# The square root moved to the head of the routing loop's turn, and the recurrent weights loaded into four buffers

## Chip, cores and metric

The kernel runs on the 8 cores of one Trainium2 chip. Times are device microseconds (us) of the slowest core. The two measured runs of the kernel before took 2318.80 and 2323.91 us, median 2321.36. The cores share no work: each computes everything that its own 2048 output rows need. Line numbers (L746) are those of the kernel file of the version spoken of.

## What is computed

One layer over x of shape (2, 8192, 1024), cut to what matters here:

```python
xn = layernorm(x)
s  = attn_block(xn)                  # linear attention, MLP with 4096 hidden columns
# slot block, on the same xn
h      = gelu(concat[xn, slot_mean] @ w1 + b1)        # 512 columns
logits = (h @ w2 + b2) / (|tau| + 0.1)                # 64 slots
alpha  = softmax over the 8 largest logits, 0 elsewhere
si = (alpha.T @ xn) / alpha.sum(0)                    # 64 x 1024 per batch
gi = si @ Wih.T + bih ; gh = S @ Whh.T + bhh          # 64 x 3072 each
S_new = GRU(gi, gh, S)
y  = layernorm(S_new + attention(S_new)) * ln_g + ln_b
slot_values = y @ wvp + bvp
g  = silu((alpha @ slot_values) @ wo + bo)
x  = x + s * g
```

`si` sums over all 8192 rows of a batch. A core therefore reads all 8192 rows, of which only the first 2048 are its own.

## The kernel before, in words

The program is a row of blocks. In a block each engine has its own hand-written list of instructions, ordered against the others by semaphores: `sdv` counts VectorE's (DVE) signals, `sac` ScalarE's (ACT), `spe` TensorE's (PE); `swA`, `swc0`, `swc1` count DMAs that GpSimd (POOL) issues. At the end of a block all engines meet.

**The routing stage** (L505 to L812) is one block with a loop over 16 tiles of 512 rows, `mt` = 0 to 15. Tiles 0 to 3 are the core's own (`own`). One turn, engine by engine:

- DVE waits for the square root of tile mt, then runs `emit_stats(mt+1)` (bn_stats and bn_aggr of the next tile, L523 to L530), `emit_apply(mt)` (reciprocal L538, then the four normalizing operations L550, into XN for own tiles, into xnb otherwise) and `emit_tail(mt-1)` (top 8, threshold mask and, after the exponentials, the weights alpha: L565 to L602). For a tile that isn't own, `emit_apply(mt)` first waits for the slot sum of tile mt-2 on PE.
- ACT runs `emit_exp(mt-1)` (L725, L734), which needs the top 8 of that tile from DVE; then `emit_sqrt(mt+1)` (L746); for own tiles four copies XN to xnb (L767); four evacuations of transposes (L777); four Gelus (L786); the copy of the logits, LOG (L795); and once per own tile a copy ALPHAT (L801), one turn late. Sqrt of tile 0 stands ahead of the loop. The loads of ACT's function tables are instructions of their own in the trace (ACT_TABLE_LOAD).
- PE transposes the tile (L675), multiplies by w1 (L689, 32 matmuls), makes the logits (L703, L709), and then sums the slots of tile mt-1 (`emit_si`, L632 to L637).
- SyncE loads tile m of x when tile m-2 has been applied.

The counts that a wait names (`a_sqrt`, `a_copy`, `aoff`, AB) are worked out ahead from the order of ACT's signals.

**The slot stage** (L862 to L1327) has 64 rows only and streams weights. Its first block (L900) only issues loads on POOL: five bias rows (`ROWB3`), slotT, wq, wk and the first two of the eight pieces of Whh, each 128 rows by 3072 columns, float32 in HBM and cast to bf16 on the way. The second block (L923) multiplies piece after piece (L944), six matmuls each, and adds the bias row (L952); POOL loads piece c into buffer c % 2 of `whb` once PE has finished piece c-2. The third block (L965) does the same with Wih (L988, L996). Three more blocks (L1125, L1218, L1276) stream wv, wvp and wo in pieces of 1024 columns.

Of the kernel before, what the change touches and what calls it, by code (L numbers as in the profile page):

```python
# [76 lines left out]
def build_nc(dbg=False):  # L77
# [51 lines left out]
    with ExitStack() as ex:  # L129
# [18 lines left out]
        sfq = E(nc.semaphore("sfq"))  # L148
        sx = [sx0, sx1]; swc = [swc0, swc1]; sfc = [sfc0, sfc1]
# [6 lines left out]
                 al1=0, fq=0)  # L156
# [29 lines left out]
        def fin(inst, sem, key):  # L186
            inst.then_inc(sem, 1)
            C[key] += 1
# [69 lines left out]
        with ExitStack() as exW:  # L258
# [6 lines left out]
            with ExitStack() as exA:  # L265
# [175 lines left out]
                t_c = 0  # L441
                a_c = 1
                for m in range(N_MT):
                    VB.append(v_c); TB.append(t_c); AB.append(a_c)
                    v_c += ((1 if m + 1 < N_MT else 0) + 4
                            + (2 if m >= 1 else 0))
                    t_c += 9 + (0 if m == 0 else
                                1 + (1 if own_f(m - 1) else 0))
                    a_c += ((0 if m == 0 else 1)
                            + (1 if m + 1 < N_MT else 0)  # L450
                            + (4 if own_f(m) else 0) + 9
                            + (1 if m >= 1 and own_f(m - 1) else 0))
# [26 lines left out]
                aoff = lambda m: ((0 if m == 0 else 1)  # L479
                                  + (1 if m + 1 < N_MT else 0)  # L480
                                  + (4 if own_f(m) else 0))
                a_sqrt = lambda m: ac0 + (1 if m == 0 else
                                          AB[m - 1]
                                          + (0 if m == 1 else 1) + 1)
                a_copy = lambda m, st: (ac0 + AB[m]
                                        + (0 if m == 0 else 1)
                                        + (1 if m + 1 < N_MT else 0)
                                        + st + 1)
# [16 lines left out]
                with nc.Block() as blk:  # L505
# [213 lines left out]
                    def _(a):  # L719
# [151 lines left out]
            with ExitStack() as exB3:  # L871
                EB = exB3.enter_context
                ROWB3 = EB(nc.sbuf_tensor("ROWB3", [1, 9216], BF16))
                slotb = EB(nc.sbuf_tensor("slotb", [64, 1024], F32))
                slotTb2 = EB(nc.sbuf_tensor("slotTb2", [128, 512], BF16))
                whb = EB(nc.sbuf_tensor("whb", [128, 6144], BF16))
# [20 lines left out]
                wslot = lambda c: whb[:, (c % 2) * 3072:(c % 2) * 3072 + 3072]  # L897
                wslot1k = lambda c: whb[:, (c % 2) * 1024:(c % 2) * 1024 + 1024]

                with nc.Block() as blk:  # L900
                    @blk.sync
                    def _(s):
                        dma(s, slotb[:], slot_d[:], sld, 'ld')

                    @blk.gpsimd
                    def _(g):
                        dmx(g, ROWB3[0:1, 0:3072], bih_rd[:], swA, 'wA')
                        dmx(g, ROWB3[0:1, 3072:6144], bhh_rd[:], swA, 'wA')
                        dmx(g, ROWB3[0:1, 6144:7168], fbv_rd[:], swA, 'wA')
                        dmx(g, ROWB3[0:1, 7168:8192], bvp_rd[:], swA, 'wA')  # L910
                        dmx(g, ROWB3[0:1, 8192:9216], fbo_rd[:], swA, 'wA')
# [11 lines left out]
                with nc.Block() as blk:  # L923
                    peS = C['pe']
                    wcB = [X['wc0'], X['wc1']]

                    @blk.gpsimd
                    def _(g):
                        for c in range(2, 8):
                            g.wait_ge(spe, peS + c - 1)  # L930
                            cast_load(g, wslot(c), whhT_d, 1, 3072,
                                      src_row0=c * 128,
                                      sem=swc[c % 2], key='wc%d' % (c % 2))

                    @blk.tensor
                    def _(t):
                        t.wait_ge(sld, ldB0)
                        t.wait_ge(swA, wA_B0)
                        for c in range(8):
                            t.wait_ge(swc[c % 2],  # L940
                                      wcB[c % 2] + 16 * (c // 2 + 1) - 16)
                            i = None
                            for jc in range(6):
                                i = t.matmul(  # L944
                                    pGH[:, jc * 512:(jc + 1) * 512],
                                    slotTb2[:, c * 64:(c + 1) * 64],
                                    wslot(c)[:, jc * 512:(jc + 1) * 512],
                                    start=(c == 0), stop=False)
                            fin(i, spe, 'pe')
                        i = None  # L950
                        for jc in range(6):
                            i = t.matmul(pGH[:, jc * 512:(jc + 1) * 512],  # L952
                                         cONE[0:1, 0:64],
                                         ROWB3[0:1, 3072 + jc * 512:
                                               3072 + (jc + 1) * 512],
                                         start=False, stop=True)
                        fin(i, spe, 'pe')
# [7 lines left out]
                with nc.Block() as blk:  # L965
                    peS = C['pe']
                    wcB2 = [X['wc0'], X['wc1']]

                    @blk.gpsimd
                    def _(g):  # L970
                        cast_load(g, wslot(0), wihT_d, 1, 3072, src_row0=0,
                                  sem=swc[0], key='wc0')
                        cast_load(g, wslot(1), wihT_d, 1, 3072, src_row0=128,
                                  sem=swc[1], key='wc1')
                        for c in range(2, 8):
                            g.wait_ge(spe, peS + c - 1)
                            cast_load(g, wslot(c), wihT_d, 1, 3072,
                                      src_row0=c * 128,
                                      sem=swc[c % 2], key='wc%d' % (c % 2))

                    @blk.tensor
                    def _(t):
                        for c in range(8):
                            t.wait_ge(swc[c % 2],
                                      wcB2[c % 2] + 16 * (c // 2 + 1))
# [7 lines left out]
                            fin(i, spe, 'pe')  # L993
                        i = None
# [130 lines left out]
                with nc.Block() as blk:  # L1125
# [4 lines left out]
                    def _(g):  # L1130
                        cast_load(g, wslot1k(0), fwv_d, 1, 1024, src_row0=0,
# [10 lines left out]
                    def _(t):  # L1142
                        for c in range(8):
# [9 lines left out]
                            fin(i, spe, 'pe')  # L1153
                        i = None
                        for nh in range(2):
                            i = t.matmul(pGH[:, nh * 512:(nh + 1) * 512],
                                         cONE[0:1, 0:64],
                                         ROWB3[0:1, 6144 + nh * 512:
                                               6144 + (nh + 1) * 512],
# [58 lines left out]
                with nc.Block() as blk:  # L1218
# [4 lines left out]
                    def _(g):  # L1223
                        cast_load(g, wslot1k(0), wvp_d, 1, 1024, src_row0=0,
# [23 lines left out]
                    def _(t):  # L1248
                        t.wait_ge(sdv, dvS + 1)
                        for c in range(8):  # L1250
# [8 lines left out]
                            fin(i, spe, 'pe')  # L1259
                        i = None  # L1260
                        for nh in range(2):
                            i = t.matmul(pGH[:, nh * 512:(nh + 1) * 512],
                                         cONE[0:1, 0:64],
                                         ROWB3[0:1, 7168 + nh * 512:
                                               7168 + (nh + 1) * 512],
# [10 lines left out]
                with nc.Block() as blk:  # L1276
# [4 lines left out]
                    def _(g):  # L1281
                        cast_load(g, wslot1k(0), fwo_d, 1, 1024, src_row0=0,
# [15 lines left out]
                    def _(t):  # L1298
                        t.wait_ge(sdv, dvS + 1)
                        for c in range(8):  # L1300
# [9 lines left out]
                            fin(i, spe, 'pe')  # L1310
                        i = None
                        for nh in range(2):
# [3 lines left out]
                                         ROWB3[0:1, 8192 + nh * 512:  # L1316
                                               8192 + (nh + 1) * 512],
# [797 lines left out]
```

## Time and profile before

| | |
|---|---|
| measured runs | 2318.80 and 2323.91 us, median 2321.36 |
| profiled execution | 2325.78 us |
| its span, slowest core (core 1) | 2324.2 us |
| spans of the eight cores | 2301.3 to 2324.2 us, granted clock 0.752 to 0.760 |
| PE busy | 1221.8 us, 53% of the span |
| DVE busy | 534.0 us, 23% |
| ACT busy | 502.8 us, 22% |
| routing loop on core 1 | about 94 to 596 us |
| slot stage on core 1 | about 600 to 858 us |

The span runs from the first to the last instruction of the slowest core. In a timeline row the first number is the start in us from the start of the span, the second the length in us, then engine, line and operation; in square brackets stand the idle time of the engine just before and what ended it. Rows with "xN" join N instructions. PEld is the weight load of TensorE. In a row of windows there stand the stretch, its length, for each engine its busy time and in brackets the number of its instructions, and at the end the granted clock as a share of 2.4 GHz, the busy share of the 16 DMA engines, and GB/s. A row of waits gives total us, how many times, and the longest.

### The profile page before, as it was taken

What the parts mean: (1) busy time and instruction counts of PE and PEld (TensorE: products, weight loads), DVE (VectorE), ACT (ScalarE), POOL (GpSimd) and SP (SyncE); (2) the same over time, 40 slices, a digit from 0 to 9 for tenths busy, and PEclk for the clock granted to TensorE, in tenths of its full rate; (3) what the DMA queues carried; (4) which work ended last, traced back from release to release, by engine and by line L of the source; (5) the groups of instructions that cost most, each with busy time, mean ns of one, the idle gap of its engine ahead of it and who ended that gap; (6) DMA issues with size and microseconds to landing.
All of it is one profiled execution on the core that took longest, in us unless ns stands there. A gap on an engine that the chain in (4) does not pass through costs nothing. (4 is left out here: it accounts for less than half of the span.)

```text
span 2324.2 us, 18897 instructions; the slowest of 8 cores (2301.3 to 2324.2 us)
## 1 busy us (share of the span) xinstructions
PE 1221.8 (53%) x6308; PEld 560.4 (24%) x6308; DVE 534.0 (23%) x1213; ACT 502.8 (22%) x747; POOL 122.3 (5%) x139
## 2 busy tenths in 40 slices
PE   0155555555243226447347348340298598697686
PEld 0022222222111002223223213210143243243342
DVE  0242333332001103233233232310400300301002
ACT  0165444444001001101001001000330521521421
POOL 1000000000100110000000000013001001001000
PEclk9977777777665557778678679575599799799798
DMA  9221212220463351512522423339809619439156
GB/s 183 52 96 60 74 49 73 73 72 1 68 120 64 51 80 40 124 38 75 105 63 68 87 64 86 68 91 135 128 1 111 142 19 110 126 37 123 58 55 91
DMA packets 341425, 183.65 MB, mean 79 GB/s; under 512 B 305171, under 2 KB 309396, under 8 KB 341332
## 3 DMA queue, kind: packets, MB, share of 16 engines
q0 software_dynamic: 182144, 72.72, 27.4%
q1 hardware_dynamic: 159188, 109.74, 16.9%
q8 instruction: 53, 0.87, 0.2%
q14 instruction: 40, 0.33, 0.0%
HBM read 204.81 MB, written 33.56 MB: 103 GB/s over the span
## 5 line engine op out<-in xcount | busy, mean ns | idle before, releaser
L689 PE MATMUL pM<-xnTs,w1ab 128*128 128x512 bf16 x512 | 150.8, 464 | 44.6 <-ACTq L191 44.5
L1937 DVE TENSOR_TENSOR y1t<-pTf,y1t 128x512 f32<-128x512 f32 x32 | 22.1, 692 | 520.1 <-PE pTf L2031 520.1
L2000 PE MATMUL pMa<-h2T,fcwb 128*128 128x512 bf16 x512 | 127.7, 394 | 19.4 <-ACTq L191 19.4
L2000 PE MATMUL pMb<-h2T,fcwb 128*128 128x512 bf16 x512 | 123.8, 386 | 0.0
L2017 PE MATMUL pPb<-g1F,pjcb 128*128 128x512 bf16 x512 | 119.2, 393 | 8.7 <-DMA pjcb<-pjw 8.5
L2017 PE MATMUL pPa<-g1F,pjcb 128*128 128x512 bf16 x512 | 113.1, 379 | 9.8 <-DMA pjcb<-pjw 4.9
L1600 ACT ACT_TABLE_LOAD x4 | 5.1, 1283 | 508.3 <-PE pBig L1553 508.3
L675 PE MATMUL pT<-cIDb,xnb 128*128 128x128 bf16 x256 | 27.5, 273 | 163.6 <-ACTq L191 148.7
L1984 PE MATMUL pT0d<-cIDb,h2b 128*128 128x128 bf16 x128 | 16.3, 307 | 159.0 <-DVEq L191 98.2
L689 PEld LDWEIGHTS pM<-xnTs,w1ab 128*128 128x128 bf16 x512 | 57.0, 115 | 134.8 <-issue 101.4
L1858 POOL DMA_DIRECT2D pjcb<-pjw x32 | 53.6, 1676 | 611.1 <-PE pPa L2017 475.7
L1437 PE MATMUL pBig<-wob,aoT 128*128 128x512 bf16 x256 | 67.5, 424 | 27.1 <-DVEq L191 27.1
L1719 PE MATMUL pBig<-FQ2h,FK2h 64*128 64x128 bf16 x256 | 31.7, 298 | 87.5 <-DMA scr_ao<-aog 78.8
L1545 PE MATMUL pBig<-wqb,xhT 128*128 128x512 bf16 x256 | 66.4, 418 | 16.4 <-ACTq L191 16.4
L550 DVE TENSOR_SCALAR xnb<-xld,ST 128x1024 bf16<-128x1024 f32 x48 | 39.0, 812 | 156.2 <-PE pDE L637 151.8
L1763 DVE TENSOR_TENSOR AMK<-pBig,cMSK 128x512 bf16<-128x512 f32 x64 | 44.3, 692 | 130.6 <-PE pBig L1719 100.3
L2000 PEld LDWEIGHTS pMa<-h2T,fcwb 128*128 128x128 bf16 x512 | 51.0, 100 | 84.0 <-issue 27.8
L2017 PEld LDWEIGHTS pPb<-g1F,pjcb 128*128 128x128 bf16 x512 | 50.8, 101 | 72.4 <-issue 19.3
L1839 POOL DMA_DIRECT2D fcwb<-fcw x32 | 28.1, 927 | 735.2 <-DMA y1scr<-XN 699.3
L2000 PEld LDWEIGHTS pMb<-h2T,fcwb 128*128 128x128 bf16 x512 | 51.1, 100 | 63.8 <-issue 6.0
L2017 PEld LDWEIGHTS pPa<-g1F,pjcb 128*128 128x128 bf16 x512 | 49.1, 98 | 70.4 <-issue 13.6
L2059 ACT ACTIVATE h2T<-pT0d,LNC 128x128 bf16<-128x128 bf16 x128 | 58.9, 460 | 27.2 <-PE pT0d L1984 15.3
(263 smaller groups left out, 1729.7 us busy)
## 6 DMA issues: line engine op xcount, KB each, us to landing
xld<-x8k SPq DMA_DIRECT2D x64, 512.0 KB, 7.0
pjcb<-pjw POOLq DMA_DIRECT2D x32, 1024.0 KB, 10.8
scr_qk<-tmb SPq DMA_DIRECT2D x16, 512.0 KB, 2.7
y1scr<-XN SPq DMA_DIRECT2D x4, 2048.0 KB, 7.2
fcwb<-fcw POOLq DMA_DIRECT2D x32, 256.0 KB, 19.1
y1t<-y1scr SPq DMA_DIRECT2D x4, 2048.0 KB, 11.2
xre<-x8k SPq DMA_DIRECT2D x16, 512.0 KB, 12.7
out<-xre SPq DMA_DIRECT2D x16, 512.0 KB, 3.2
```

Source lines behind the costliest of these rows:

```text
L550: i = v.tensor_scalar(dstx, xs, ST[:, pb + 2 * st:pb + 2 * st + 1], ST[:, rd + st:rd + st + 1], ALU.subtract, ALU.mult)
L675: i = t.transpose(dstb[:, cc * 128:(cc + 1) * 128], xb[:, cc * 128:(cc + 1) * 128], cIDb[:])
L689: i = t.matmul(dstp[:, 0:512], w1ab[:, cc * 512 + ch * 128: cc * 512 + (ch + 1) * 128], xnTs[:, cc * 512:(cc + 1) * 512], start=(cc == 0), ...
L1437: i = t.matmul(pBig0[:, nh * 512:(nh + 1) * 512], aoT[:, cc * 128:(cc + 1) * 128], wob[:, cc * 1024 + nh * 512: cc * 1024 + (nh + 1) * 512 ...
L1545: i = t.matmul(pBig0[:, nh * 512:(nh + 1) * 512], xhT[:, cc * 512 + st * 128: cc * 512 + (st + 1) * 128], wqb[:, cc * 1024 + nh * 512: cc ...
L1719: i = t.matmul(pBig0[:, (b % 2) * 512 + gl * 128: (b % 2) * 512 + (gl + 1) * 128], FK2h[0:64, g * 128:(g + 1) * 128], FQ2h[0:64, g * 128:( ...
L1763: i = v.tensor_tensor(AMK[:, (b % 2) * 512:(b % 2 + 1) * 512], pBig0[:, (b % 2) * 512:(b % 2 + 1) * 512], cMSK[:], ALU.mult)
L1839: g.dma_start(out=dstap, in_=srcap).then_inc(sfc[q % 2], 16)
L1858: g.dma_start(out=dstap, in_=srcap).then_inc(spj[slot], 16)
L2000: i = t.matmul(dstp[:, :], fcwb[:, m * 1024 + cc * 128: m * 1024 + (cc + 1) * 128], h2T[:, cc * 512:(cc + 1) * 512], start=(cc == 0), stop ...
L2017: i = t.matmul(dstp[:, :], pjcb[:, (d % 2) * 4096 + m * 128: (d % 2) * 4096 + (m + 1) * 128], g1F[:, m * 512:(m + 1) * 512], start=(m == 0 ...
L2059: i = a.activation(h2T[:, cc * 512 + st * 128: cc * 512 + (st + 1) * 128], pT0d[:, cc * 128:(cc + 1) * 128], AF.Identity, bias=LNC[:, 24 + ...
```

## The change

In the routing stage ACT no longer computes the square root of the next tile between the exponentials and the evacuations. It computes that of the tile of the current turn, ahead of `emit_exp(mt-1)`. The counts are adapted to it. DVE's, PE's and SyncE's lists stay as they are.

In the slot stage `whb` holds four pieces of 3072 columns where it held two (with two more semaphores, `sxt0` and `sxt1`), and `ROWB3` shrinks from 9216 to 3072 columns. The first block loads one bias row and four pieces of Whh; the four other bias rows are each loaded at the head of the block that uses them, and PE waits for them ahead of the bias matmuls. The three streams of 1024-column pieces keep two buffers.

```diff
@@ routing stage, ACT
-                        def emit_sqrt(m):
-                            a.wait_ge(sdv, v_aggr(m))
-                            pb = P_(m); sd = SD_(m)
+                        for mt in range(N_MT):
+                            own = own_f(mt)
+                            par = mt % 2
+                            a.wait_ge(sdv, v_aggr(mt))
+                            pb = P_(mt); sd = SD_(mt)
                             i = a.activation(
...
-                        emit_sqrt(0)
-                        for mt in range(N_MT):
-                            own = own_f(mt)
-                            par = mt % 2
                             if mt >= 1:
                                 emit_exp(mt - 1)
-                            if mt + 1 < N_MT:
-                                emit_sqrt(mt + 1)
@@ slot stage, buffers
-                wslot = lambda c: whb[:, (c % 2) * 3072:(c % 2) * 3072 + 3072]
+                wslot = lambda c: whb[:, (c % 4) * 3072:
+                                      (c % 4) * 3072 + 3072]
+                swc4 = [swc0, swc1, sxt0, sxt1]
@@ first block
-                        dmx(g, ROWB3[0:1, 0:3072], bih_rd[:], swA, 'wA')
-                        dmx(g, ROWB3[0:1, 3072:6144], bhh_rd[:], swA, 'wA')
...
+                        dmx(g, ROWB3[0:1, 0:3072], bhh_rd[:], swA, 'wA')
...
-                        cast_load(g, wslot(0), whhT_d, 1, 3072, src_row0=0,
-                                  sem=swc[0], key='wc0')
-                        cast_load(g, wslot(1), whhT_d, 1, 3072, src_row0=128,
-                                  sem=swc[1], key='wc1')
+                        for c0 in range(4):
+                            cast_load(g, wslot(c0), whhT_d, 1, 3072,
+                                      src_row0=c0 * 128,
+                                      sem=swc4[c0], key=wk4[c0])
@@ second block
-                        for c in range(2, 8):
-                            g.wait_ge(spe, peS + c - 1)
+                        for c in range(4, 8):
+                            g.wait_ge(spe, peS + c - 3)
@@ third block
+                        dmx(g, ROWB3[0:1, 0:3072], bih_rd[:], swA, 'wA')
+                        for c in range(4):
                             cast_load(g, wslot(c), wihT_d, 1, 3072,
                                       src_row0=c * 128,
...
+                        t.wait_ge(swA, X['wA'])
@@ blocks of wv, wvp, wo, each with its own row
+                        dmx(g, ROWB3[0:1, 0:1024], fbv_rd[:], swA, 'wA')
```

ACT's order in the routing stage, before, from the logits of tile 5 to those of tile 6 (L746 is the square root, L725 and L734 the exponentials, L777 the evacuations, L786 the Gelus):

```order
L795 ACTIVATE LOG<-pLb 128x256
L725 ACTIVATE E<-TKS,ST,SCAL 128x8 x4
L734 ACTIVATE etk<-LOG,ST,SCAL 128x64 x4
L746 ACTIVATE ST<-ST,SCAL 128x4
L777 ACTIVATE xnTs<-pT 128x8x128
L777 ACTIVATE xnTs<-pM 128x8x128 x2
L777 ACTIVATE xnTs<-pT 128x8x128
L786 ACTIVATE hFs<-pM,B1E 128x512 x4
L795 ACTIVATE LOG<-pLa 128x256
```

The same stretch in the changed kernel, with its own line numbers (L742 is the square root, L719 and L728 the exponentials):

```order
L784 ACTIVATE LOG<-pLb 128x256
L742 ACTIVATE ST<-ST,SCAL 128x4
L719 ACTIVATE E<-TKS,ST,SCAL 128x8 x4
L728 ACTIVATE etk<-LOG,ST,SCAL 128x64 x4
L766 ACTIVATE xnTs<-pT 128x8x128
L766 ACTIVATE xnTs<-pM 128x8x128 x2
L766 ACTIVATE xnTs<-pT 128x8x128
L775 ACTIVATE hFs<-pM,B1E 128x512 x4
L784 ACTIVATE LOG<-pLa 128x256
```

The square root moved from behind the exponentials to ahead of them, and it is now that of tile 6, the tile whose normalization follows, where before it was that of tile 7.

POOL's order at the start of the slot stage, before (an UNCONDITIONAL_BRANCH marks the entry or the end of a block):

```order
L905 UNCONDITIONAL_BRANCH
L183 DMA ROWB<-bih_r 1x16x192
L183 DMA ROWB<-bhh_r 1x16x192
L183 DMA ROWB<-fbv_r 1x16x64
L183 DMA ROWB<-bvp_r 1x16x64
L183 DMA ROWB<-fbo_r 1x16x64
L200 DMA slotTb<-slotT 128x8x64
L200 DMA fwqb<-fwq 128x8x256
L200 DMA fwkb<-fwk 128x8x256
L200 DMA whb<-whhT 128x3072 x2
L900 UNCONDITIONAL_BRANCH
L927 UNCONDITIONAL_BRANCH
```

And now:

```order
L897 UNCONDITIONAL_BRANCH
L184 DMA ROWB<-bhh_r 1x16x192
L201 DMA slotTb<-slotT 128x8x64
L201 DMA fwqb<-fwq 128x8x256
L201 DMA fwkb<-fwk 128x8x256
L201 DMA whb<-whhT 128x3072 x4
L892 UNCONDITIONAL_BRANCH
L915 UNCONDITIONAL_BRANCH
```

Four bias rows left the first block, and two more pieces of Whh stand in it, ahead of the place where the engines meet.

## Rows read from the trace of the kernel before

**Rows 1.** The longest waits, whole program: who waited, for whom, us, times, longest.

```profile
DVE xnb L550 <- PE pDE L637: 151.8, 12, 17.1
```

**Rows 2.** Windows from the logits of one tile to those of a later one.

```profile
129.78:219.82 90.04, 47.41 (x285) 25.22 (x286) 31.59 (x95) 55.78 (x78) 0.00 (x0) 0.72 0.20 71
219.82:279.72 59.90, 32.34 (x201) 16.37 (x200) 23.24 (x66) 29.12 (x45) 0.00 (x0) 0.74 0.21 71
279.72:556.82 277.10, 149.49 (x865) 72.82 (x864) 99.28 (x285) 125.72 (x189) 0.00 (x0) 0.73 0.19 61
```

**Rows 3.** Timeline of ACT, one turn of the routing loop (tile 8).

```profile
341.68 0.39 ACT L795 ACTIVATE LOG<-pLb 128x256 f32<-128x256 f32 x1 [1.89 <-PE pLb L709]
348.70 1.28 ACT L725 ACT_TABLE_LOAD   x1 [6.64 <-DVEq L191]
...
352.72 1.28 ACT L746 ACT_TABLE_LOAD   x1
...
354.47 1.02 ACT L777 ACTIVATE xnTs<-pT 128x1024 bf16<-128x1024 bf16 x1 [0.16 <-issue]
...
371.86 0.39 ACT L795 ACTIVATE LOG<-pLa 128x256 f32<-128x256 f32 x1 [1.89 <-PE pLa L709]
```

**Rows 4.** Timeline of DVE in the same turn.

```profile
343.63 3.62 DVE L550 TENSOR_SCALAR xnb<-xld,ST 128x1024 bf16<-128x1024 f32 x4 [11.54 <-PE pDE L637]
...
356.97 0.69 DVE L523 BATCH_NORM_STATS2 ST<-xld 128x6 f32<-128x512 f32 x1 [1.10 <-ACTq L191]
```

**Rows 5.** Timeline of ACT and DVE at the first tile.

```profile
101.06 0.30 ACT L746 ACTIVATE ST<-ST,SCAL 128x4 f32<-128x4 f32 x1
101.61 0.69 DVE L523 BATCH_NORM_STATS2 ST<-xld 128x6 f32<-128x512 f32 x1 [1.95 <-ACTq L191]
...
107.32 0.81 DVE L550 TENSOR_SCALAR XN<-xld,ST 128x1024 f32<-128x1024 f32 x1
```

**Rows 6.** Timeline of ACT, own tile 2: logits, ALPHAT copy, first copy.

```profile
158.57 0.39 ACT L795 ACTIVATE LOG<-pLb 128x256 f32<-128x256 f32 x1 [1.73 <-PE pLb L709]
160.76 0.59 ACT L801 ACTIVATE ALPHAT<-pT 64x512 bf16<-64x512 bf16 x1 [1.81 <-PE pT L644]
...
167.32 1.06 ACT L767 ACTIVATE xnb<-XN 128x1024 bf16<-128x1024 f32 x1 [0.21 <-issue]
```

**Rows 7.** Timeline of POOL in the slot stage.

```profile
600.63 0.49 POOL L183 DMA_DIRECT2D ROWB<-bhh_r  x1
...
630.91 0.53 POOL L200 DMA_DIRECT2D whb<-whhT  x1 [24.57 <-PE pGH L944]
...
673.64 1.05 POOL L200 DMA_DIRECT2D whb<-wihT  x2 [15.68 <-DVEq L965]
```

**Rows 8.** Timeline of PE in the slot stage.

```profile
627.61 4.41 PE L944 MATMUL pGH<-whb,slotTb 128*64 128x512 bf16 x12 [28.84 <-PEq L900]
...
667.90 1.48 PE L952 MATMUL pGH<-ROWB,cONE 1*64 1x512 bf16 x6
682.05 2.74 PE L988 MATMUL pGH<-whb,siTb 128*64 128x512 bf16 x6 [12.67 <-DMA whb<-wihT]
686.79 2.74 PE L988 MATMUL pGH<-whb,siTb 128*64 128x512 bf16 x6 [2.01 <-DMA whb<-wihT]
...
723.82 2.76 PE L996 MATMUL pGH<-ROWB,cONE 1*64 1x512 bf16 x6
```

**Rows 9.** Timeline of all engines at the block behind the slot stage.

```profile
858.83 0.90 POOL L200 DMA_DIRECT2D wob<-wo  x1 [7.55 <-PEq L1379]
...
876.10 0.69 DVE L234 BATCH_NORM_STATS2 ST<-XN 128x6 f32<-128x512 f32 x1 [18.07 <-PEq L1379]
```

**Rows 10.** DMA issues: KB and us to landing.

```profile
wob<-wo POOLq DMA_DIRECT2D x1, 2048.0 KB, 15.8
```

**Rows 11.** Timeline of PE, the matmuls by w1 in one turn.

```profile
359.58 9.60 PE L689 MATMUL pM<-xnTs,w1ab 128*128 128x512 bf16 x32 [2.92 <-ACTq L191]
...
360.39 0.15 PEld L689 LDWEIGHTS pM<-xnTs,w1ab 128*128 128x128 bf16 x1 [0.28 <-issue]
```

More of the change, by code:

```diff
@@ L148, in build_nc @@
         sfq = E(nc.semaphore("sfq"))
+        sxt0 = E(nc.semaphore("sxt0")); sxt1 = E(nc.semaphore("sxt1"))
         sx = [sx0, sx1]; swc = [swc0, swc1]; sfc = [sfc0, sfc1]
@@ L440, in build_nc @@
                 v_c = 1
-                t_c = 0
-                a_c = 1
+                t_c = a_c = 0
                 for m in range(N_MT):
@@ L478, in build_nc @@
                 t_alphat = lambda m: pe0 + TB[m + 1] + 11
-                aoff = lambda m: ((0 if m == 0 else 1)
-                                  + (1 if m + 1 < N_MT else 0)
+                aoff = lambda m: (1 + (0 if m == 0 else 1)
                                   + (4 if own_f(m) else 0))
[L482 to L488, printed above, removed]
+                a_sqrt = lambda m: ac0 + AB[m] + 1
+                a_copy = lambda m, st: (ac0 + AB[m] + 1
+                                        + (0 if m == 0 else 1) + st + 1)
                 a_evac = lambda m, st: ac0 + AB[m] + aoff(m) + st + 1
@@ L924, in build_nc @@
                     peS = C['pe']
-                    wcB = [X['wc0'], X['wc1']]
+                    wcB = [X[k] for k in wk4]
                     @blk.gpsimd
                     def _(g):
-                        for c in range(2, 8):
-                            g.wait_ge(spe, peS + c - 1)
+                        for c in range(4, 8):
+                            g.wait_ge(spe, peS + c - 3)
                             cast_load(g, wslot(c), whhT_d, 1, 3072,
                                       src_row0=c * 128,
-                                      sem=swc[c % 2], key='wc%d' % (c % 2))
+                                      sem=swc4[c % 4], key=wk4[c % 4])
                     @blk.tensor
@@ L939, in _ @@
                         for c in range(8):
-                            t.wait_ge(swc[c % 2],
-                                      wcB[c % 2] + 16 * (c // 2 + 1) - 16)
+                            t.wait_ge(swc4[c % 4],
+                                      wcB[c % 4] + 16 * (c // 4))
                             i = None
@@ L966, in build_nc @@
                     peS = C['pe']
-                    wcB2 = [X['wc0'], X['wc1']]
+                    wcB2 = [X[k] for k in wk4]
                     @blk.gpsimd
                     def _(g):
[L971 to L976, printed above, removed]
+                        dmx(g, ROWB3[0:1, 0:3072], bih_rd[:], swA, 'wA')
+                        for c in range(4):
                             cast_load(g, wslot(c), wihT_d, 1, 3072,
                                       src_row0=c * 128,
-                                      sem=swc[c % 2], key='wc%d' % (c % 2))
+                                      sem=swc4[c], key=wk4[c])
+                        for c in range(4, 8):
+                            g.wait_ge(spe, peS + c - 3)
+                            cast_load(g, wslot(c), wihT_d, 1, 3072,
+                                      src_row0=c * 128,
+                                      sem=swc4[c % 4], key=wk4[c % 4])
                     @blk.tensor
@@ L983, in _ @@
                         for c in range(8):
-                            t.wait_ge(swc[c % 2],
-                                      wcB2[c % 2] + 16 * (c // 2 + 1))
+                            t.wait_ge(swc4[c % 4],
+                                      wcB2[c % 4] + 16 * (c // 4 + 1))
                             i = None
@@ L1153, in _ @@
                             fin(i, spe, 'pe')
+                        t.wait_ge(swA, X['wA'])
                         i = None
@@ L1259, in _ @@
                             fin(i, spe, 'pe')
+                        t.wait_ge(swA, X['wA'])
                         i = None
@@ L1310, in _ @@
                             fin(i, spe, 'pe')
+                        t.wait_ge(swA, X['wA'])
                         i = None
```

31 lines of the change are left out of this document (15 added, 16 removed).

## Prediction

> **What bounds the kernel now.** I read the table of cores first: the eight spans lie within 1%, so one core stands for all, and no core waits for another. The page's shares say little, since each stage has its own limit; the change touches two, the routing loop and the slot stage, so I went to the waits. The longest wait of DVE in the routing loop is 151.8 us, twelve times ahead of the normalization L550, for the slot sum on PE [rows 1]. It looks like slack, and the change is about what is in that slack.
>
> Next the windows: nine turns from tile 5's logits to tile 14's take 277.10 us, 30.79 each [rows 2], while in them PE is busy 149.5 us, ACT 125.7 and DVE 99.3. None is full. The turn is a chain through all three. Followed in one turn: logits copied at 341.68; DVE starts to normalize at 343.63, released by PE's slot sum; ACT's table load for the exponentials starts at 348.70, released by DVE (the top 8 of the tail stand behind the normalization in DVE's list); then comes the square root's table load at 352.72, and the first evacuation at 354.47, then transposes, matmuls, Gelus, and the next logits at 371.86 [rows 3, 4]. That is 30.18 us. The reader is to see two things in it. The next tile's statistics start at 356.97, behind the tail, and run beside the matmuls by w1: they cost nothing. And the square root stands on the chain, from 352.72 to 354.47, 1.75 us.
>
> The slot stage is bound by loads: its PE rows wait for DMA between pieces [rows 8].
>
> **The routing stage.** The square root of tile mt now stands behind the logits of tile mt-1 in ACT's list. DVE's list is unchanged: it waits for that root, and *then* does the statistics of tile mt+1, the normalization of mt, and the tail of mt-1. Queued behind the new wait are therefore the statistics, which were hidden, and with them the tail, the exponentials on ACT and all that follows. From the start of the logits copy to the start of the normalization the chain becomes:
>
> 0.39 (the copy) + 0.16 (issue) + 1.28 (table load) + 0.02 + 0.55 (from the root's start to DVE's start of the statistics, 101.06 to 101.61) + 5.71 (statistics to normalization, 101.61 to 107.32) = 8.11 us [rows 3, 5].
>
> Before it was 343.63 - 341.68 = 1.95 us, so 6.16 longer. The root leaves its old place, which gives back 1.75. Net 4.41 us a turn, and 30.18 + 4.41 = 34.59 us for a turn.
>
> - Tiles 6 to 14, nine turns: 9 x 34.59 = 311.3 against 277.1, so +34.2. (Some turns before took longer than 30.18 as their mean of 30.79 shows; where that comes from a later slot sum, it is now covered by the statistics, so I don't add to those.)
> - Tiles 4 and 5: the ALPHAT copy stands ahead of the root. It ends at 160.76 + 0.59 = 161.35, 2.78 us after the logits' start instead of 0.39 [rows 6]. That is 2.39 more, so 4.41 + 2.39 = 6.8 each: +13.6 against the 59.9 us of those two turns [rows 2].
> - Own tiles 2 and 3: before, statistics and normalization of the tile ran ahead in the previous turn, so the way from logits to the first copy was only 167.32 - 158.57 = 8.75 us [rows 6]. Now it is 8.11 + 2.39 to the normalization, + 5.07 to the table load of the exponentials (343.63 to 348.70) + 4.02 through them (348.70 to 354.47, less 1.75) = 19.59 [rows 3, 4]. +10.84 each, 21.7. Tile 1 has no ALPHAT copy ahead; I take 1.2 off for it, half of 2.39, since before part of that copy was hidden: +9.6. Together +31.3, on the 90.04 us of these three turns.
> - Tile 15 has no next tile: no statistics, no root given back. Logits to normalization is 0.39 + 0.16 + 1.28 + 0.02 + 0.55 + 0.25 for the reciprocal (an estimate) = 2.65 instead of 1.95: +0.7. Tile 0 is as before.
>
> Sum: 34.2 + 13.6 + 31.3 + 0.7 = **+79.8 us**. One table load more in all (the first two roots shared one) is within it. x arrives earlier than needed: SyncE loads tile m when m-2 is normalized, and its statistics now start a whole turn later. Bounds: the delays of the chain are read from rows, but the clock of the 32 matmuls by w1 is not fixed; they take 9.60 us [rows 11], and a turn with a different pause ahead of them may take 1 us less or more. 15 turns: 65 to 95.
>
> **The slot stage.** In the third block two loads are issued at 673.64 and their pieces used at 682.05 and 686.79: 8.4 us to the first and 4.74 for the next, with the queue never empty [rows 7, 8]. With four in the queue I take 4.74 for each that follows. The block then runs 673.64 + 0.5 (bias row's issue, 0.49 [rows 7]) + 8.4 + 7 x 4.74 + 2.74 + 2.76 = 721.2, against 723.82 + 2.76 = 726.6: -5.4.
>
> The Trainium skill bears on the 4.74, in DMA: Bandwidth & Descriptors, section "Anatomy of one DMA — SWDGE (gpsimd) path": about 2.0 us and then the bytes at 436 GB/s. By it 1.5 MB would move in 3.6 us, and the block would gain 8 us more. The trace's 4.74 decides here.
>
> In the first block, what releases PE? PE starts both pieces 0 and 1 in one run of 12 matmuls at 627.61, released by the end of the block, not by one piece [rows 8]. And the block behind the slot stage shows the same: wo is issued at 858.83 and lands 15.8 us later, at 874.6, and only then, at 876.10, does DVE leave the block, though its next work needs no wo [rows 9, 10]. So a block's end waits for the loads that POOL issued in it. Then four pieces in the first block hold all engines for two pieces more: 627.61 + 2 x 4.74 - 1.95 (four fewer bias rows at 0.49) = 635.1. POOL issued piece 2 3.3 us after PE's start (630.91); now that is piece 4, at 638.4, into an empty queue. It lands 8.4 later, three more follow at 4.74: 661.0. Then 2.74 + 2.76 at the lower clock, or about half of it at the higher (667.90 shows 1.48): 665.2 in the middle, against 669.38: -4.2. If the end of the block did not wait, the eight pieces would stream through and the gain would be some 12; if loads in the same queue hinder each other, nothing. The three later blocks each issue a bias row first: 3 x 0.5 = +1.5.
>
> Slot stage: -5.4 - 4.2 + 1.5 = **-8.1 us**, bounds -20 and +2. PE, which waits for bias rows now, waits for what landed long before.
>
> **Sum.** 2325.8 (the profiled execution; span 2324.2 and 1.6 around it) + 79.8 - 8.1 = 2397.5. This execution lay 4.4 above the median of the runs, so against the median I take a little less: **2395 us**, 3.2% slower. What can be told from no change is about 2% (46 us).
>
> **Rivals.**
>
> 1. *The clock stays low.* PE's pause ahead of a turn's work grows by 4 to 11 us. In the row of the 32 matmuls the weight loads early in the row come 0.43 us apart (0.15 + 0.28), yet the row takes 9.60, so the clock rises within it. Were it not to rise any more, 32 x 0.43 = 13.8, 4.2 more in 15 turns: +63, **2458 us**. For: the granted clock is only 0.73 in these turns [rows 2, 11]. Against: the pause ahead of these matmuls themselves, from transposes to evacuations, hardly changes. The Trainium skill, TensorE: Matmul & The Clock Gate, section "HAM oscillation — how this bites in real kernels", says that a wait between bursts sends the array back to half rate and each burst starts cold; the trace agrees that each of these turns starts cold already, and so that rule speaks for no new loss.
> 2. *The end of a block doesn't wait for loads*, and PE starts piece 0 when it lands. Then the second block gains 12 instead of 4: **2387 us**. For: piece 0 has its own semaphore. Against: rows 9.
> 3. *Faster.* DVE's 151.8 us ahead of L550 swallow the statistics, and only the root's 1.75 us leave the chain. Place: the gap from the end of the statistics to the normalization. Price: 14 x 1.75 = 24.5 saved, with the slot stage's 8.1: **2293 us**. It decides if the root's result reaches DVE 5.7 us before the slot sum ends. For: the idle time is there, 11.5 us in a turn [rows 4]. Against: ACT reaches the root only after the logits copy, which starts 1.95 us before the slot sum is through, so DVE cannot use the idle time. I see no way round that in ACT's list.
> 4. *Less than it looks*: own tiles hide part of it (DVE's or ACT's slack elsewhere) and the slot stage gains 20: 2325.8 + 60 - 20 = **2366 us**, just within 2%.
>
> **How the numbers follow.** My forecast 0.79, rival 1 0.06, rival 2 0.09, rival 3 0.02, rival 4 0.04. The range of the forecast is 65 to 95 and -20 to +2 around 2321 to 2326, where both ends at once are unlikely: 2372 to 2418, and it takes rival 2 in; rivals 1, 3 and 4 are left out, 0.12, and with the tails of the forecast under 0.2. Slower by over 2% (above 2367.8): forecast, rivals 1 and 2, 0.94; within 2%: rival 4, 0.04; faster: rival 3, 0.02.
>
> **What would show it.** In the trace after, the turn from logits to logits is 34 to 35 us for tiles 6 to 14 (30.8 on average before); the root's table load starts right behind the logits copy; the statistics follow it at once; the idle time ahead of L550's successor for the slot sum is gone, and a DVE wait for ACT of some 15 us ahead of the statistics stands in its place; the slot stage starts near 680. PE starts Whh's piece 0 some 35 us after the stage begins (27.5 before), with four pieces in one run, and the third block's pieces come about 4.7 us apart. I am wrong if the statistics still run beside the matmuls, if the 32 matmuls take over 11 us, or if PE starts Whh's first piece before the fourth has landed.

## The result, and the profile after

The changed kernel is slower: 2.8% over the kernel before, ratio 1.028 with a 95% interval of 1.0248 to 1.0313. The median of its eleven runs is 2392.99 us, against 2323.34 for ten runs of the kernel before. In some executions the cores of one die show a lower granted clock and the time is longer (one run of the changed kernel took 2458.40 us, at 0.72 on one die where 0.75 is usual); the medians count such runs and the ratios leave them out, which is why 2392.99 / 2323.34 is a little more than 1.028. The profiled execution took 2391.08 us, its span on the slowest core (core 3) is 2389.5 us.

The spans of both kernels split at two points that every core passes once: POOL's first load of the slot stage and its load of wo. The table is worked out from the POOL and PE timelines of each of the eight cores. The columns are: start of the slot stage; from there to PE's first matmul of Whh; from there to the last matmul of the Whh block; length of the Wih block; from its end to the load of wo; the whole slot stage.

```
                          start   PE first  Whh end  Wih block  rest    slot stage
before            mean   600.19    25.74     68.19     49.84   131.89     254.19
                  range  598-603   24-27     66-72     46-53   131-133    249-259
changed kernel    mean   675.46    33.08     62.04     45.02   133.64     244.99
                  range  672-679   32-35     59-65     43-47   132-135    241-249
```

So the routing stage ends 75.3 us later and the slot stage is 9.2 us shorter. Behind the load of wo, 1465.4 us were left on the slowest core before (858.83 to 2324.2) and 1465.5 are left now (924.03 to 2389.5). Nothing came from there.

First the windows of the changed kernel on core 3, from logits to logits, the same stretches as [rows 2]. Columns as there.

```profile
130.60:252.09 121.49, 48.13 (x285) 25.36 (x286) 34.84 (x99) 55.76 (x78) 0.00 (x0) 0.65 0.15 52
252.09:325.52 73.43, 33.89 (x201) 18.15 (x200) 23.24 (x66) 29.12 (x45) 0.00 (x0) 0.67 0.17 58
325.52:633.76 308.24, 149.78 (x865) 78.00 (x864) 104.57 (x297) 125.72 (x189) 0.00 (x0) 0.71 0.16 55
```

The three own turns take 31.45 us more, tiles 4 and 5 13.5, the nine turns behind them 31.1. PE's and ACT's instructions are the same in number. DVE has 4 more in the first window and 12 more, the statistics of one tile, in the third, since the statistics now fall into another turn. Busy times grew by 5.3 us or less in each window: this is waiting, not work. Now one turn, on ACT (it answers to [rows 3]):

```profile
394.33 0.38 ACT L784 ACTIVATE LOG<-pLb 128x256 f32<-128x256 f32 x1 [1.89 <-PE pLb L703]
394.85 1.28 ACT L742 ACT_TABLE_LOAD   x1
396.15 0.30 ACT L742 ACTIVATE ST<-ST,SCAL 128x4 f32<-128x4 f32 x1
407.48 1.28 ACT L719 ACT_TABLE_LOAD   x1 [11.04 <-DVEq L192]
...
411.52 1.03 ACT L766 ACTIVATE xnTs<-pT 128x1024 bf16<-128x1024 bf16 x1 [0.15 <-issue]
...
428.73 0.39 ACT L784 ACTIVATE LOG<-pLa 128x256 f32<-128x256 f32 x1 [1.89 <-PE pLa L703]
```

and on DVE, which answers to [rows 4]:

```profile
396.69 0.69 DVE L517 BATCH_NORM_STATS2 ST<-xld 128x6 f32<-128x512 f32 x1 [17.89 <-ACTq L192]
...
402.15 0.18 DVE L532 RECIPROCAL ST<-ST 128x4 f32<-128x4 f32 x1
402.41 3.62 DVE L544 TENSOR_SCALAR xnb<-xld,ST 128x1024 bf16<-128x1024 f32 x4
406.27 0.61 DVE L559 MAX8 TKS<-LOG 128x8 f32<-128x64 f32 x4 [0.24 <-issue]
```

Read them together. The root's table load follows the logits at once, the root is done at 396.45, DVE starts the statistics at 396.69 and the normalization at 402.41. That is 8.08 us after the logits' start; it was 1.95. ACT then has nothing to do for 11.04 us, waiting for the tail behind the normalization; before, it waited 6.64. The wait of DVE for the slot sum has left the list of long waits, and in its place stands the wait of DVE for ACT ahead of the statistics:

```profile
DVE ST L517 <- ACTq L192: 280.0, 15, 25.1
```

That is 151.8 us of waiting turned into 280.0. It now ends ahead of work that used to be hidden.

In the slot stage, PE (answering to [rows 8]) on the same core:

```profile
711.99 8.21 PE L932 MATMUL pGH<-whb,slotTb 128*64 128x512 bf16 x24 [36.27 <-PEq L892]
724.25 2.38 PE L932 MATMUL pGH<-whb,slotTb 128*64 128x512 bf16 x6 [4.05 <-DMA whb<-whhT]
728.79 2.74 PE L932 MATMUL pGH<-whb,slotTb 128*64 128x512 bf16 x6 [2.16 <-DMA whb<-whhT]
733.04 1.46 PE L932 MATMUL pGH<-whb,slotTb 128*64 128x512 bf16 x6 [1.51 <-DMA whb<-whhT]
736.69 1.46 PE L932 MATMUL pGH<-whb,slotTb 128*64 128x512 bf16 x6 [2.20 <-DMA whb<-whhT]
738.08 1.48 PE L940 MATMUL pGH<-ROWB,cONE 1*64 1x512 bf16 x6
753.46 2.74 PE L977 MATMUL pGH<-whb,siTb 128*64 128x512 bf16 x6 [13.90 <-DMA whb<-wihT]
```

Four pieces are multiplied in one run of 24 matmuls, 34.9 us after the stage's first load at 677.08. The row names PE's own sequencer at the end of the first block (L892) as what released them, and no DMA: PE was held by the block's end.

### The profile page after: what moved, and what is told of

It reads as the page before. It is cut to its first block and busy times, and to the rows that moved or that the text cites. A ratio compares the mean times of both kernels' runs of the same rounds, so it can differ in the third digit from the quotient of the medians.

```text
span 2389.5 us, 18898 instructions; the slowest of 8 cores (2360.1 to 2389.5 us)
## 1 busy us (share of the span) xinstructions
PE 1225.1 (51%) x6308; PEld 568.4 (24%) x6308; DVE 534.0 (22%) x1213; ACT 503.9 (21%) x748; POOL 122.5 (5%) x139
## 5 line engine op out<-in xcount | busy, mean ns | idle before, releaser
L517 DVE BATCH_NORM_STATS2 ST<-xld 128x6 f32<-128x512 f32 x64 | 43.6, 681 | 280.6 <-ACTq L192 280.0
L1433 PE MATMUL pBig<-wob,aoT 128*128 128x512 bf16 x256 | 72.7, 448 | 27.3 <-DVEq L192 27.3
L669 PEld LDWEIGHTS pT<-cIDb,xnb 128*128 128x128 bf16 x256 | 24.5, 137 | 250.9 <-issue 250.9
L1541 PE MATMUL pBig<-wqb,xhT 128*128 128x512 bf16 x256 | 64.2, 408 | 16.1 <-ACTq L192 16.1
L1996 PEld LDWEIGHTS pMa<-h2T,fcwb 128*128 128x128 bf16 x512 | 51.0, 100 | 84.0 <-issue 27.6
```

What stands on the lines that cost most here:

```text
L517: v.bn_stats(ST[:, SB[st]:SB[st] + 6], xslot(mt, st)[:, 0:512])
L669: i = t.transpose(dstb[:, cc * 128:(cc + 1) * 128], xb[:, cc * 128:(cc + 1) * 128], cIDb[:])
L1433: i = t.matmul(pBig0[:, nh * 512:(nh + 1) * 512], aoT[:, cc * 128:(cc + 1) * 128], wob[:, cc * 1024 + nh * 512: cc * 1024 + (nh + 1) * 512 ...
L1541: i = t.matmul(pBig0[:, nh * 512:(nh + 1) * 512], xhT[:, cc * 512 + st * 128: cc * 512 + (st + 1) * 128], wqb[:, cc * 1024 + nh * 512: cc ...
L1996: i = t.matmul(dstp[:, :], fcwb[:, m * 1024 + cc * 128: m * 1024 + (cc + 1) * 128], h2T[:, cc * 512:(cc + 1) * 512], start=(cc == 0), stop ...
```

## The experiments

Each kernel but one, which was run once, was compared with the kernel before on the same chip. The first two take the change apart.

**The routing part alone.** The edit is the first part of the diff on the kernel before.

> Only the routing part of the change (the root of tile mt ahead of the exponentials), with the slot stage of before. Theory (the statistics are queued behind the root's wait): the routing stage is 77 us longer, as in the changed kernel's trace, turns of tiles 6 to 14 at 34.1 to 34.6 us, the slot stage as before (258.7 us from its first load to the load of wo): about 2402 us, ratio 1.033. Rival (part of the loss comes from an interplay with the slot stage's loads, or the loss is not the routing stage's): under 2390 us.

Measured: ratio 1.0297, 1.0253 to 1.0341; profiled execution 2400.51 us. The slot stage starts at 676.60 in the mean of eight cores, 76.4 later than before, and takes 253.3 (before 254.2). The nine turns:

```profile
322.50:630.54 308.04, 149.98 (x865) 78.10 (x864) 104.49 (x297) 125.51 (x190) 0.00 (x0) 0.71 0.15 55
```

The same as in the changed kernel (308.24). The whole loss is here, and it doesn't depend on the slot stage's loads.

**The slot part alone.** The edit is the rest of the diff.

> Only the slot part of the change (four buffers, bias rows moved), with the routing stage of before. Theory: the slot stage is 8 to 12 us shorter (the prediction's term is 8.1, the changed kernel's trace shows 11.8): 2312 to 2317 us, ratio 0.995 to 0.9965. Rival (a start of the stage at another time or state is what made it faster): no change, ratio 1.000.

Measured: ratio 0.997, 0.9937 to 1.0002, which by itself is not told from 1; profiled execution 2317.32 us. Its slot stage is 245.4 us in the mean of eight cores, range 241 to 250, against 249 to 259 before: 8.8 us shorter, with the start unmoved at 600.3. So the stage is faster by what was expected, also from a start that did not move, and its rival falls. The total's interval takes in both the 0.9965 expected and no change. The first two kernels' effects add up to the changed kernel's: 76.4 - 8.8 = 67.6, measured 66.1 (75.3 - 9.2) at the load of wo.

**What costs: the statistics, or the root's place?** ACT's list stays that of the changed kernel; two statements of DVE are swapped.

```diff
                         for mt in range(N_MT):
-                            v.wait_ge(sac, a_sqrt(mt))
                             if mt + 1 < N_MT:
                                 emit_stats(mt + 1)
+                            v.wait_ge(sac, a_sqrt(mt))
                             emit_apply(mt)
```

> The changed kernel with two statements of DVE swapped: the statistics of tile mt+1 ahead of the wait for the root of tile mt. ACT's order stays that of the changed kernel. Theory (what costs is the statistics behind that wait, not the root's place): in a turn of tiles 6 to 14 the logits-to-normalization way falls from 8.1 to 2.65 us, the turn to 28.8 to 29.2 us, own tiles stay 4 to 5.5 us longer than before; in all +4 against the kernel before in the routing stage and -12 in the slot stage: about 2317 us, ratio 0.9965. Rival (the root's table load or its place ahead of the exponentials is what costs): stays above 2370 us.

Measured: ratio 0.997, 0.9935 to 1.0006; profiled execution 2322.74 us. The windows, own tiles 1 to 3, tiles 4 and 5, tiles 6 to 14:

```profile
127.55:232.00 104.45, 48.41 (x285) 25.53 (x286) 34.83 (x99) 55.68 (x78) 0.00 (x0) 0.67 0.18 61
232.00:293.99 61.99, 33.44 (x201) 17.51 (x200) 23.22 (x66) 29.05 (x44) 0.00 (x0) 0.72 0.20 68
293.99:555.83 261.84, 148.08 (x865) 73.99 (x864) 99.24 (x285) 125.44 (x189) 0.00 (x0) 0.72 0.21 65
```

and one turn on DVE:

```profile
365.68 0.69 DVE L517 BATCH_NORM_STATS2 ST<-xld 128x6 f32<-128x512 f32 x1 [1.29 <-DMA xld<-x8k]
...
382.42 0.18 DVE L532 RECIPROCAL ST<-ST 128x4 f32<-128x4 f32 x1 [11.40 <-ACTq L192]
382.67 3.62 DVE L544 TENSOR_SCALAR xnb<-xld,ST 128x1024 bf16<-128x1024 f32 x4
```

The statistics again run beside the matmuls by w1, and DVE's wait stands behind them. Turns of tiles 6 to 14 take 29.09 us, even less than before the change (30.79), since the root is off the way from exponentials to evacuations. Own turns stay 14.4 us longer in all than before, 4.8 each (4 to 5.5 were expected), because there the normalization too had run a turn ahead. The slot stage starts at 602.7 in the mean of eight cores, 2.5 later than in the kernel before and 72.8 earlier than in the changed kernel. Two statements of DVE undo nearly all of the loss, with ACT's order as changed. The rival falls.

**Does a block's end wait for the loads POOL issued in it?** Two kernels, both on the changed one. In the first no end stands between the first loads and the matmuls:

```diff
                 with nc.Block() as blk:
+                    peS = C['pe']
+                    wcB = [X[k] + 16 for k in wk4]
...
                         for c0 in range(4):
                             cast_load(g, wslot(c0), whhT_d, 1, 3072,
...
-                with nc.Block() as blk:
-                    peS = C['pe']
-                    wcB = [X[k] for k in wk4]
-
-                    @blk.gpsimd
-                    def _(g):
                         for c in range(4, 8):
```

> The changed kernel with the first block of the slot stage merged into the second, so that no end of block stands between the first loads and the matmuls. Theory (a block's end waits for all loads that POOL issued in it): PE starts Whh's first piece 21 to 25 us after the stage's first load instead of 34.9, the pieces come about 4.7 apart, the last matmul of the block ends at 57 to 60 instead of 62.5 us: 2386 us, some 3 to 5 under the changed kernel. Rival (no such wait; loads land late by themselves): PE's first piece at 35 us as in the changed kernel, same time.

```profile
694.54 2.74 PE L928 MATMUL pGH<-whb,slotTb 128*64 128x512 bf16 x6 [21.27 <-DMA whb<-whhT]
699.17 2.74 PE L928 MATMUL pGH<-whb,slotTb 128*64 128x512 bf16 x6 [1.89 <-DMA whb<-whhT]
704.14 1.62 PE L928 MATMUL pGH<-whb,slotTb 128*64 128x512 bf16 x6 [2.23 <-DMA whb<-whhT]
708.27 2.74 PE L928 MATMUL pGH<-whb,slotTb 128*64 128x512 bf16 x6 [2.51 <-DMA whb<-whhT]
...
728.11 1.48 PE L936 MATMUL pGH<-ROWB,cONE 1*64 1x512 bf16 x6
```

On this core (core 1) the stage's first load is at 674.64. PE's first matmul comes 19.9 us after it, 20.3 in the mean of eight cores (range 18 to 24; 33.1 with the block's end), now released by the piece itself, and the next pieces come 4 to 5 us apart. The fourth is used 33.6 us after the first load, 34.0 in the mean. That is where the changed kernel starts all four at once (33.1), as it must if the block's end waits until the fourth has landed. The Whh block ends at 55.5 instead of 62.0, the slot stage takes 239.3 instead of 245.0: 5.7 less, more than the 3 to 5 I had expected. The total, ratio 1.0215 with 1.0144 to 1.0286, overlaps the changed kernel's, so the total alone doesn't tell the two apart.

In the second, both blocks and their end stay; of the four pieces two are issued at the head of the second block:

```diff
-                        for c0 in range(4):
+                        for c0 in range(2):
...
-                        for c in range(4, 8):
-                            g.wait_ge(spe, peS + c - 3)
+                        for c in range(2, 8):
+                            if c >= 4:
+                                g.wait_ge(spe, peS + c - 3)
```

> The changed kernel, but of the four pieces of Whh that the first block loads two move to the head of the second block, so that the two blocks and their end stay and only what is in flight at that end changes. Theory (the end waits for what POOL issued before it): PE starts Whh's first piece two pieces earlier than in the changed kernel, 23 to 25 us after the stage's first load instead of 33.1 (mean of eight cores), and the block ends at 59 to 62 instead of 62.0: the total barely moves. Rival (PE starts late because loads of the same queue hold each other up, not because of the block's end): the first piece still starts past 31 us, since the same four pieces are queued.

```profile
678.11 1.13 POOL L201 DMA_DIRECT2D whb<-whhT  x2
698.94 4.32 PE L934 MATMUL pGH<-whb,slotTb 128*64 128x512 bf16 x12 [25.35 <-PEq L892]
698.95 1.07 POOL L201 DMA_DIRECT2D whb<-whhT  x2 [19.71 <-ACTq L911]
702.23 0.53 POOL L201 DMA_DIRECT2D whb<-whhT  x1 [2.21 <-PE pGH L934]
```

POOL itself is held at the block's end for 19.71 us (this is core 6) and then issues the next two; PE starts at the same time, with the two pieces in one run. That is 22.9 us after the stage's first load in the mean of eight cores, 10.2 earlier than with four pieces ahead of the end. By itself this run doesn't refute the rival: the third and fourth piece are only issued when PE starts, so they could not hold up the first. The run before does: there all four are issued in one go, and the first is used after 20.3 us. It is the end that holds, not the queue. The Whh block ends at 58.2, a bit better than the 59 to 62 expected and 3.9 better than with four: here the loads put ahead of a block's end make PE and POOL wait for them. The total was taken once (2390.76 us) and does not tell it from the changed kernel.

**Taking the root off the chain as well.** In the kernel before the root stood on the chain and the statistics did not. Neither needs to be on it: behind the four evacuations ACT idles for 3.9 us, and the root goes there:

```diff
                             if mt >= 1:
                                 emit_exp(mt - 1)
-                            if mt + 1 < N_MT:
-                                emit_sqrt(mt + 1)
...
                                 finv(a, sac, 'ac')
+                            if mt + 1 < N_MT:
+                                emit_sqrt(mt + 1)
                             for ch in range(4):
                                 a.wait_ge(spe, t_h(mt, ch))
```

On the kernel before, with its slot stage:

> The kernel before with only the root moved behind the evacuations, slot stage as before. Theory: 14 x 1.75 = 24.5 us less, 2300 us, ratio 0.9895. Rival (hidden time comes back as a wait of DVE or PE): same time as before.

Measured: ratio 0.9867, 0.9828 to 0.9906. The slot stage starts at 575.8 in the mean of eight cores, 24.4 earlier than before; 24.5 was worked out. The rival falls.

With four buffers and the merged block too:

> The root of tile mt+1 moved behind the four evacuations of tile mt, where ACT idles for 3.9 us until the first matmuls by w1 are done; DVE's list as before; the slot stage with four buffers and its first two blocks merged. Theory (in the kernel before the root's 1.75 us were on the chain and the statistics were not; here neither is): turns of tiles 6 to 14 at 28.4 to 29.1 us, the routing stage 20 to 26 us shorter than before, the slot stage 15 shorter (254.2 to 239.3 in means of eight cores): 2282 to 2292 us, ratio 0.985. Rival (the root there delays the first Gelu, or the statistics then come too late for the normalization): the routing stage is no shorter than before, ratio 0.993.

```profile
343.97 1.02 ACT L774 ACTIVATE xnTs<-pT 128x1024 bf16<-128x1024 bf16 x1 [0.16 <-issue]
345.14 1.28 ACT L745 ACT_TABLE_LOAD   x1
346.43 0.30 ACT L745 ACTIVATE ST<-ST,SCAL 128x4 f32<-128x4 f32 x1
348.92 1.28 ACT L785 ACT_TABLE_LOAD   x1 [2.19 <-PE pM L688]
```

The root and its table load sit in ACT's idle time, of which 2.19 us are left ahead of the Gelus' table load. The nine turns take 260.02 us, 28.9 each. Ratio 0.9824, 0.9786 to 0.9861; the slot stage starts at 574.8 and takes 238.1, 25.4 and 16.1 better than before. The rival falls here too.

**The three later streams.** On top of that kernel, whose label is e6_root_hidden, each stream of eight loads becomes two loads of four pieces:

```diff
-                        cast_load(g, wslot1k(0), fwv_d, 1, 1024, src_row0=0,
-                                  sem=swc[0], key='wc0')
...
-                        for c in range(2, 8):
-                            g.wait_ge(spe, peS + c - 1)
...
+                        for hf in range(2):
+                            cast_load(g, whb, fwv_d, 4, 1024,
+                                      dst_off=hf * 4096, src_row0=hf * 512,
+                                      sem=swc[hf], key='wc%d' % hf)
```

> As e6_root_hidden, and the three streams of 1024-column pieces are each loaded by two DMAs of four pieces, issued at the head of their block, instead of eight DMAs of which six wait for PE. Theory (these blocks are bound by the round trip of issue, landing and matmul, not by bytes): the wvp block gets some 17 us shorter, the other two 4 to 5 each, 20 to 28 us in all under e6_root_hidden: 2258 to 2270 us, ratio 0.975. Rival (they are bound by HBM bandwidth): no gain over e6_root_hidden.

```profile
738.00 1.53 POOL L201 DMA_DIRECT2D whb<-wvp  x2
760.83 0.52 POOL L184 DMA_DIRECT2D ROWB<-fbo_r  x1 [21.30 <-ACTq L1266]
```

In the kernel before, on core 1:

```profile
788.61 1.05 POOL L200 DMA_DIRECT2D whb<-wvp  x2 [17.81 <-ACTq L1218]
795.44 0.53 POOL L200 DMA_DIRECT2D whb<-wvp  x1 [5.78 <-PE pGH L1255]
...
831.27 1.05 POOL L200 DMA_DIRECT2D whb<-fwo  x2 [8.05 <-ACTq L1276]
```

Measured: ratio 0.966, 0.9612 to 0.9708, median of eight runs 2256.48 us. From the end of the Wih block to the load of wo it takes 96.8 us in the mean, against 133.2 in the kernel just above: 36.4 less, more than the 20 to 28 I had worked out. The bytes are the same, so the rival falls. The wvp block takes 23.3 us from its first load to the next block's bias row (core 2; 21.3 in the mean of eight cores), where before it took 42.7 from first load to first load. This version beats both kernels.

The wvp block owes much of that to something else. In the kernel before and in the changed one POOL waits there for `peS + c` ahead of piece c, where the blocks of wv and wo wait for `peS + c - 1`: one piece later than two buffers need, so its second buffer never gets ahead. In e6_root_hidden the way from a block's first load to the end of its bias matmuls is 25.5 us for wv, 40.0 for wvp and 25.5 for wo; here it is 19.0, 18.2 and 17.8 (means of eight cores). Some 14.5 of the 36.4 us would by this come from that one count (an estimate, 40.0 - 25.5; no run changes the count alone).

## Why the prediction was right

2395 was predicted and 2392.99 measured, within the range. That the totals lie within 2 us of each other is in part luck. The difference between the kernels was forecast as 79.8 - 8.1 = 71.7 us; it is 66.1 at the load of wo (75.3 - 9.2), 65.3 between the two profiled executions and 69.7 between the medians of all runs, and the ratio is 2.8% where 3.2% was forecast. The mechanism held in each term. By its steps:

- **The new wait and what stands behind it** held. Logits to normalization was worked out at 8.11 us and measured at 8.08; with the 11.04 us of ACT's idle time, logits to exponentials is 13.15 where 8.11 + 5.07 = 13.18 was forecast. That the statistics are the cost was only argued in the prediction; swapping two statements of DVE shows it.
- **Own tiles** +31.3, measured 31.45. **Tiles 4 and 5** +13.6, measured 13.5. **Tile 15** +0.7: 28.20 us in the trace after (633.76 to 661.96), 27.99 before (556.82 to 584.81), so +0.2.
- **Tiles 6 to 14** were mis-sized a little: +34.2, measured 31.1. The mean turn after is 34.25, 34.59 was forecast. The way from logits to exponentials was right; the rest of the turn was taken too long. From the exponentials' table load to the next logits the turn used as the base gives 371.86 - 348.70 - 1.75 = 21.41 us; in the trace after the same way is 21.25 in the turn shown and 20.96 in the next (441.87 to 462.83), whose 32 matmuls take 9.41 us instead of 9.60. The base of 30.18 was well chosen although the mean was 30.79. Before, five of the nine turns take 30.2 to 30.3 us and four take 31.3 to 31.7. In those four the slot sum runs at the lower clock (granted 0.55 from 309.80 to 313.60, against 1.00 from 371.70 to 373.80), and the normalization starts 3.4 to 3.5 us after the logits instead of 1.96. After the change it starts 8.08 us after them in all nine: the statistics cover the later slot sum, as the prediction said in brackets.
- **The slot stage** -8.1, measured 9.2 shorter in the mean of eight cores. Its parts: Wih block -5.4, measured -4.8; Whh block -4.2, measured -6.2; later blocks +1.5, measured +1.75 (131.89 to 133.64). The later start was right: PE's first piece came 33.08 - 25.74 = 7.3 us later in the mean, 7.5 was forecast (34.9 us after the first load on core 3, 35.0 forecast). What was too long is the way from there to the end of the block, 30.1 us forecast and 29.0 measured in the mean, 27.6 on core 3. On that core the first piece reloaded takes 8.96 us from its issue at 715.29 to its use, a little more than the 8.4 taken; the next three come 4.15 us apart instead of 4.74; and the last piece and the bias take 2.87 us at the higher clock, where the middle of both clocks, 4.1, had been taken. The kernel before took 42.5 us for that way in the mean, 41.8 on the core used for the forecast. In the third block of core 3 the pieces come 4.58 us apart on average.
- **The block's end.** PE's release by the end of the block was read from [rows 8 to 10] and is now shown by two kernels. Rival 2 gave 0.09 to the other way, and it is refuted; its price was right all the same: with the end gone, the Whh block ends 12.7 us earlier than in the kernel before (68.2 to 55.5), 12 had been put.
- **Rival 1, a clock that stays low**, didn't happen: the 32 matmuls take 9.42 us in the turn from 394.33, and PE's clock in the nine turns is 0.71 where it was 0.73. **Rival 3** is refuted by the trace: DVE can't use its idle time while the root comes first. **Rival 4** needed both a smaller loss and a larger gain; the loss was within 4.5 us of its sum (75.3 against 79.8).

One step of the text had a wrong number beside a right mechanism: a DVE wait for ACT of "some 15 us ahead of the statistics" is 17.5 to 25.1 us (280.0 us in 15 waits). It stood outside the sum.

## What to carry to other kernels

An instruction that takes 0.3 us put 6.1 us into each turn's chain here (1.95 to 8.08), because another engine waits for it ahead of work that does not need it; before moving it, list what is queued behind each of its waits, on the engine that waits. Put such a small instruction, with its table load, where its engine idles anyway, and put the wait directly ahead of the first instruction that needs the result. Here the loads that POOL issues ahead of a block's end are waited for at that end: deeper prefetch across it delays the first use, while inside a block more and larger loads in flight paid. And check the count that a refill waits for against the number of buffers: one too high, and a buffer stands idle.

## What the runs showed that I had not expected

- In the kernels with four buffers, preloading more was worse than preloading less: with two pieces ahead of the block's end the Whh block ended at 58.2 us, with four at 62.0, with no end at all at 55.5 (means of eight cores).
- Two loads of 1024 KB (as written to SBUF) with nothing waiting between them carried the wvp block in 21.3 us, where eight of 256 KB, six of them issued only after the piece before had been multiplied, took 42.7 (means of eight cores). Where the refill waited one piece less, for wv and wo, the gain was 6.4 and 7.8 us.
- The slot stage of the same code differs by up to 10 us between cores of one execution (249 to 259 us before). One core's trace would have been too little to judge a gain of 9; the means of eight cores agree within 2.3 us between executions of the same slot code (254.2, 253.3, 251.9).
- The first transposes of a turn ran at 1.2 GHz after the change where they had run at 2.4: eight of them take 1.01 us at 403.51 after (granted clock 0.50), 0.61 at 344.74 before (1.00). PE had idled 7.39 us ahead of them instead of 1.27. It cost nothing, since the normalization that feeds them is as slow.
